# Layer-norm normalisation moved from VectorE to ScalarE, its bias made on GpSimd, under a new hand-fixed order of all engines' steps

## The reference

```python
# block 0, 16 heads of 8, EPS = 1e-5
z  = _mha(x, x, Wq1, Wk1, Wv1, mask0, causal=True)
x1 = _layernorm(x + z, ln1_g, ln1_b)
z  = _mha(x1, context, Wq2, Wk2, Wv2, mask1, causal=False)
x2 = _layernorm(x1 + z, ln2_g, ln2_b)
z  = jnp.maximum(x2 @ fc1_w.T + fc1_b, 0.0) * mask0
z  = (z @ fc2_w.T + fc2_b) * mask0
x3 = _layernorm(x2 + z, ln3_g, ln3_b)
# block 1, 16 heads of 64, eps = 1e-6; keys and values from the context
scores = qh / sqrt(dk) @ kh.T + bias + graph_attn_bias
out = softmax(scores) @ vh @ wo + bo + x3
out = (out - mu) * rsqrt(var + 1e-6) * ln_g + ln_b
```

## Time and profile before

| | |
|---|---|
| median of 3 runs | 377.48 us (376.44 to 379.8) |
| the profiled execution, its own time | 376.83 us |
| span of the profiled execution (first to last instruction) | 375.0 us |
| mean granted TensorE clock | 0.991 of full |
| busy: PE, PEld, DVE, ACT, POOL | 93%, 70%, 78%, 64%, 64% of the span |

### The profile page before, as it was taken

The page is one execution under the profiler, slowest core; times in us unless marked ns, Lnnn a source line. Parts: engine busy times, 40 slices in busy tenths (PEclk is TensorE's granted clock), DMA queues, the critical chain, the costliest instruction groups (busy, mean ns, idle before and its releaser), DMA issues.

```text
span 375.0 us, 13323 instructions
## 1 busy us (share of the span) xinstructions
PE 348.3 (93%) x5375; PEld 261.8 (70%) x5383; DVE 291.5 (78%) x836; ACT 241.2 (64%) x567; POOL 240.0 (64%) x376
## 2 busy tenths in 40 slices
PE   7588989999999999999999999999999897999998
PEld 3255547677878777777878787877688685777765
DVE  3456887898879988979889897889787966787551
ACT  1317556586767767586768776777768575577641
POOL 0243272848485859677686959596868667777763
PEclk9969999999999999999999999999999999999999
DMA  5992000020100022100102000023010010110000
GB/s 167 352 301 105 2 2 3 2 59 2 58 3 2 3 66 63 58 4 10 59 10 66 2 9 3 2 66 121 2 56 13 2 66 9 58 54 16 9 9 16
DMA packets 13181, 17.88 MB, mean 48 GB/s; under 512 B 1601, under 2 KB 10177, under 8 KB 13121
## 3 DMA queue, kind: packets, MB, share of 16 engines
q1 hardware_dynamic: 13120, 17.04, 14.7%
HBM read 15.99 MB, written 1.05 MB: 45 GB/s over the span
## 4 chain that ended last, share of the span: by engine, by line
PE 66%; DVE 9%; ACT 8%; POOL 7%; issue 5%; SPq 2%; DMA 1%; ACTq 0%; POOLq 0%; DVEq 0%
PE C_E L545 6%; PE C_E L600 6%; PE C_E L561 4%; PE C_E L590 4%; PE A_E L407 3%; PE B_E L407 3%; PE A_E L426 3%; PE C_E L577 3%; PE B_E L329 3%; PE A_E L440 2%; PE B_E L426 2%; PE C_E L502 2%; ACT qT L731 1%; PE B_J L369 1%; PE B_E L440 1%
## 5 line engine op out<-in xcount | busy, mean ns | idle before, releaser
L1039 POOL TENSOR_TENSOR Sc<-Sc,C_mx 128x512 f32<-128x512 f32 x28 | 29.1, 1043 | 33.0 <-DVE C_mx L947 33.0
L989 POOL TENSOR_TENSOR A_kblk<-A_qk,cst 128x1024 f32<-128x1024 f32 x16 | 30.3, 1896 | 17.4 <-DVE A_qk L833 17.4
L731 ACT ACTIVATE qT<-C_E,bq 128x128 f32<-128x128 f32 x112 | 31.7, 370 | 13.6 <-PE C_E L545 13.6
L999 POOL TENSOR_TENSOR L_rstd<-L_ve,cst 128x1 f32<-128x1 f32 x64 | 35.1, 549 | 5.0
L997 POOL TENSOR_TENSOR L_ve<-L_mv,cst 128x1 f32<-128x1 f32 x64 | 12.1, 189 | 39.4 <-DVE L_mv L898 38.9
L1010 POOL TENSOR_TENSOR L_xg<-L_xh,vec_sb 128x128 f32<-128x128 f32 x64 | 29.3, 458 | 11.9 <-DVE L_xh L907 11.7
L989 POOL TENSOR_TENSOR B_kblk<-B_qk,cst 128x1024 f32<-128x1024 f32 x16 | 30.3, 1897 | 2.6 <-DVE B_qk L833 2.4
L545 PE MATMUL C_E<-x3T,wq_sb 128*128 128x128 f32 x224 | 31.2, 283 | 0.0
L1048 POOL TENSOR_TENSOR Pc<-Pc,C_rd 128x512 f32<-128x512 f32 x28 | 28.9, 1042 | 2.1 <-DVE C_rd L957 1.8
L600 PE MATMUL C_E<-wo_sb,C_zT 128*128 128x128 f32 x224 | 27.9, 278 | 1.1 <-DVE Sc L937 1.1
L545 PEld LDWEIGHTS C_E<-x3T,wq_sb 128*128 128x128 f32 x224 | 27.1, 191 | 1.5 <-issue 0.6
(11 more groups left out here) (179 smaller groups left out, 1021.9 us busy)
## 6 DMA issues: line engine op xcount, KB each, us to landing
f<-in_fs SPq DMA_DIRECT2D x16, 512.0 KB, 3.7
out<-osb SPq DMA_DIRECT2D x16, 64.0 KB, 1.6
xTs<-in_xT SPq DMA_DIRECT2D x1, 768.0 KB, 9.2
xs<-in_x SPq DMA_DIRECT2D x1, 768.0 KB, 11.1
cs<-in_ctxn SPq DMA_DIRECT2D x1, 768.0 KB, 12.8
cTs<-in_ctxT SPq DMA_DIRECT2D x1, 768.0 KB, 9.3
vec_sb<-in_vecs SPq DMA_DIRECT2D x1, 640.0 KB, 6.7
wk_sb<-in_wk SPq DMA_DIRECT2D x1, 512.0 KB, 4.2
```

The source lines that it names most:

```text
L731: last = act.activation(place(n).qT[:, 4 * g + j], place(n).E[g][:, j * P:(j + 1) * P], ACT.Identity, bias=bq8[:, 4 * g + j:4 * g + j + 1] ...
L989: tt(a.kblk[:], a.qk[:, 1].unsqueeze(1).to_broadcast([P, 8, P]), at["rmask"].unsqueeze(2).to_broadcast([P, 8, P]), ALU.mult).then_inc(a.s_ ...
L999: tt(l.rstd[:], l.ve[:], at["power"], ALU.pow).then_inc(l.s_rstd, 1)
L1039: tt(v, v, place(n).mx[:, 8 * g:8 * g + 8].unsqueeze(2).to_broadcast([P, 8, S]), ALU.subtract).then_inc(C.s_sub, 1)
```

## The change

The instruction that writes `xh` goes from DVE (`tensor_scalar`, subtract and multiply) to ACT (`activation` Identity with `scale = rstd` and `bias = nb`, both one value a partition). POOL makes the bias `nb = -mean * rstd` with one more small `tensor_scalar` behind its power, so its `rstd` step has three instructions and two waits on itself. POOL's power now waits for the `xh` of the pair before (it overwrites `rstd`), and DVE's `bn_aggr` waits for `nb` of the pair before. All the numbers of `TURN`, `SHIFT` and `MOVES` are new, so the order of every engine is new. The sort that makes `PLAN` is the same.

```diff
-            l.rstd = sb(name + "_rstd", [P, 1])
+            l.rstd, l.nb = sb(name + "_rstd", [P, 1]), sb(name + "_nb", [P, 1])
...
+            def xh(l):
+                def step(n):
+                    act.wait_ge(l.s_nb, n + 1)
+                    if n:
+                        act.wait_ge(l.s_xg, n)
+                    act.activation(l.xh[:], l.y, ACT.Identity, bias=l.nb[:, 0:1], scale=l.rstd[:, 0:1]).then_inc(l.s_xh, 1)
+                return step
...
                     if n:
-                        dve.wait_ge(l.s_rstd, 2 * n)
+                        dve.wait_ge(l.s_nb, n)
                     dve.bn_aggr(l.mv[:], l.st[:]).then_inc(l.s_st, 1)
-                return step
-
-            def xh(l):
-
-                def step(n):
-                    dve.wait_ge(l.s_rstd, 2 * n + 2)
-                    if n:
-                        dve.wait_ge(l.s_xg, n)
-                    ts(l.xh[:], l.y, l.mv[:, 0:1], l.rstd[:, 0:1], ALU.subtract, ALU.mult).then_inc(l.s_xh, 1)
                 return step
...
                     pool.wait_ge(l.s_rstd, 2 * n + 1)
+                    if n:
+                        pool.wait_ge(l.s_xh, n)
                     tt(l.rstd[:], l.ve[:], at["power"], ALU.pow).then_inc(l.s_rstd, 1)
+                    pool.wait_ge(l.s_rstd, 2 * n + 2)
+                    ts(l.nb[:], l.mv[:, 0:1], l.rstd[:, 0:1], -1.0, ALU.mult, ALU.mult).then_inc(l.s_nb, 1)
                 return step
...
 TURN = """
-C.loadf=-26.883018006 C.store=-24.459548631 A.m0=-21.572682671 C.chi=-21.300857442 A.q0=-21.027749677
...
+K.warm=-66.189258692 C.whi=-59.455516873 C.wlo=-59.255277783 C.wvhi=-59.135367780 C.wvlo=-57.917225969
...
```

More of the change, by code:

```diff
@@ L179, in norm @@
             l.g, l.b, l.eps = vec[g], vec[b], eps
-            l.s_y, l.s_st, l.s_rstd, l.s_xh, l.s_xg, l.s_out = (
-                sem(name + "_" + s) for s in ("y", "st", "rstd", "xh", "xg", "out"))
+            l.s_y, l.s_st, l.s_rstd, l.s_nb, l.s_xh, l.s_xg, l.s_out = (
+                sem(name + "_" + s) for s in ("y", "st", "rstd", "nb", "xh", "xg", "out"))
             return l
@@ L755, in _ @@
                           nm + ".pts_0": pts(a, 0), nm + ".pts_1": pts(a, 1), nm + ".zts": zts(a)}
+            for k, l in (("A.", L1), ("B.", L2), ("B.3", L3), ("C.", L4)):
+                steps[k + "xh"] = xh(l)
             for g in range(2):
@@ L1072 @@
[L1072 to L1076, removed]
@@ L1087 @@
[L1087 to L1091, removed]
@@ new lines @@
+A.exp_1=-39.698980284 A.pt_0=-39.667170504 A.pt_1=-39.658426251 A.pts_0=-39.638358855 A.pts_1=-39.600689991
+A.pv_0=-39.550192019 A.pv_1=-39.505916818 A.zts=-39.479086357 C.k_0=-39.446620085 A.z=-39.420641251
+C.k_1=-39.397056866 C.ks_0=-39.386896501 C.ks_1=-39.355475904 A.y=-39.321858204 A.zn=-39.317639179
+A.st=-39.310154048 A.rstd=-39.253970807 A.xh=-39.145167601 A.gb=-38.979284281 B.cm=-38.500757520
+B.am=-38.483341845 B.tr=-38.305750131 B.xts=-38.262265725 B.qkv=-38.199907432 B.qk=-38.116663204
@@ new lines @@
+B.q0=-38.091499286 B.e0=-38.048938760 B.nz=-38.010955691 B.kblk=-37.999682825 B.cnt=-37.996832504
+B.cut=-37.958768552 B.v=-37.939922381 B.e=-37.784331587 B.max_0=-37.711340297 B.max_1=-37.697541882
+B.sub_0=-37.580379120 B.exp_0=-37.537418189 B.sub_1=-37.509380313 B.pt_0=-37.451145024 B.exp_1=-37.392169028
+B.pts_0=-37.376336410 B.pt_1=-37.330301725 B.pts_1=-37.291316697 B.pv_0=-37.226953932 B.pv_1=-37.213538689
+B.zts=-37.159859668 B.z=-37.120087902 B.zn=-37.016758988 B.y=-36.929493284 B.st=-36.876877648
@@ new lines @@
+C.fadd_0=-35.588498098 C.fadd_1=-35.565807876 C.max_0=-35.496566190 C.max_1=-35.448586860 C.sub_0=-35.444034645
+C.exp_0=-35.431102929 C.sub_1=-35.429612334 C.den_0=-35.319434976 C.nrm_0=-35.259262406 C.exp_1=-35.126969617
+C.den_1=-35.044441179 C.nrm_1=-34.941040892 C.pt_0=-34.891067718 C.pt_1=-34.891065205 C.store=-34.876879236
+C.pts_0=-34.862841496 C.pts_1=-34.793893943 C.zt=-34.771699169 C.zts_0=-34.731963894 C.zts_1=-34.690611021
+C.x3c=-34.645927740 C.o=-34.488828892 C.y=-34.385194498 C.st=-33.868785586 C.rstd=-33.751024413
@@ new lines @@
+L.warm#15=-11.098535410 A.qk#0=-23.498690921 A.qk#1=-19.802708301 A.qk#2=-19.763909938 A.qk#3=-20.224541021
+A.qk#4=-20.714710629 A.qk#5=-20.478036018 A.qk#6=-20.803214884 A.qk#7=0.230631446 A.qk#8=0.146274171
+A.qk#9=0.028211108 A.qk#10=0.130327158 A.qk#11=0.193589234 A.qk#12=0.070960346 A.qk#13=0.083425166
+A.qk#14=-0.049249739 A.qk#15=-0.046536786 C.whi#0=-0.117880345 C.whi#1=-0.224082744 C.whi#2=-0.323722276
+C.whi#3=0.100084020 C.whi#4=0.038962993 C.whi#5=0.001183341 C.whi#6=-0.009074067 C.whi#7=0.092005951
```

897 lines of the change are left out of this document (448 added, 449 removed).

## The result

The changed kernel takes 394.39 us (median of 4 runs, 392.6 to 397.53) where the kernel before takes 377.74 in the same comparison (4 runs, 376.44 to 379.8): a ratio of 1.0445 with a 95% interval of 1.0363 to 1.0526. It is 16.7 us slower. I had forecast 372.9 us, and a range up to 380.

The account below looks back on a forecast made before the run. The prediction took PE's own work to bound the middle, DVE next. Start -1.5, middle -4.0 and end +0.9 made -4.6 us: 372.2 for the profiled execution, 372.9 us for the median, range 368.5 to 380.

Parts of the forecast that it names:

- What bounds the kernel: Whole run: PE's own work bounds the middle, busy 195.8 of 200 us, with DVE next.
- The relief of DVE: DVE: 64 xh instructions taken away, 25 us of its 291.5 us busy time.
- Added on ACT and POOL: ACT: 64 ACTIVATEs of 0.47 us, 30 us at most; POOL: 64 nb of 0.19 us, 17 us with gaps.
- The latency of a norm: Each norm, variance to xh: 0.34 us longer, plus what stands before it in ACT's queue.
- the two waits that look back one pair: Power for the last xh, aggregate for the last nb: costed at nothing, in the middle and near the last pairs.
- Rival (b): ACT's and POOL's queues take over, PE waits 16 x 0.34 = 5.4 us for chain B's xh: 382.3 us; chance 0.15.
- The start, -1.5: Start, to 84.85 us: some six places gain 0.1 to 0.5 us each, 1.5 us taken; bounds 0 and 2.8.
- The middle, -4.0: Middle, 11 periods: relieved DVE and periodic order remove the irregular part, a gain of 4.0 us; bounds 0 and 5.3.
- the likeliest case: Whole run: the forecast's own case, gain of 7.6 to 2.5 us, 369.9 to 375.0 us; chance 0.48.
- rival (d): Order worse by 0.2 us a period, DVE's relief pays: 376.9 us; chance 0.27, shared with the rival of a hidden gain.
- The end, +0.9: End, from 308.23 us: three longer norms +1.0, more idle products +0.4, B.nz earlier -0.5: 0.9 us longer.
- rival (c): Start, 19 to 25 us: the drop to half clock goes too, giving 370.5 us; chance 0.10.

Follow-up runs that it names:

- dve_xh_late: Kernel before with 55 of the 64 xh one place later in VectorE's own queue, nothing else changed: 390.36 us, ratio 1.0328.
- edit_alone: The edit (xh on ScalarE, nb on GpSimd) under the order of the kernel before, only xh given places in ScalarE's queue: 394.21 us, ratio 1.0418.
- order_alone: New order on every engine with the code of the kernel before, xh on VectorE at places chosen by the author: 391.75 us, ratio 1.0328.
- act_no_nb: Kernel before's order, xh moved to ScalarE, no nb (constant bias, mean not subtracted): 390.0 us, ratio 1.0313.
- dve_after_nb: As pool_nb, but VectorE's xh waits for nb and uses it: 388.59 us, ratio 1.0269.
- pool_nb: Kernel before's code and order, GpSimd also makes the 64 nb, awaited only by the same norm's next aggregate: 382.08 us, ratio 1.0112.
- act_l2: Kernel before's order; only norm L2 (after attention B) has xh on ScalarE and nb on GpSimd: 383.94 us, ratio 1.0197.
- new_start: Kernel before's code, steps grouped in the new order's three pieces, only the first in the new order inside: 385.59 us, ratio 1.0206.
- act_l4: Kernel before's order; only the fourth norm (before the output) has xh on ScalarE and nb on GpSimd: 378.69 us, ratio 1.003.
- new_end: Kernel before's code, steps grouped in the new order's three pieces, only the last in the new order inside: 381.6 us, ratio 1.0111.

## Why the prediction was wrong, step by step

**What bounds the kernel.** "The middle of the run is bound by PE's own work", with DVE next, was read from shares. PE's share was right and the conclusion from it wasn't. dve_xh_late adds no work to any engine and is 12.7 us longer; so PE's 98% is the outcome of an order and no cushion in which a norm's delay is lost. "PE itself waited for xh hardly at all there: 0.2 us" is the same error. I read a wait of nothing as slack. It only says that PE wasn't made to wait, with that order, by that `xh`; it gives no figure for how much later `xh` may come, and none for the steps that stand behind it in its engine's queue.

**The relief of DVE.** I had 25 us off and 266 us left; it is 274.8, so 16.7 off. The 64 durations do add up to 25. But instructions of one engine overlap in the trace: the `xh` at 52.34 lasts to 52.75 and `A_mx` behind it began at 52.67, so what an `xh` takes up is less than its duration. With the order held fixed it is 0.29 to 0.30 us: DVE has 272.8 us in edit_alone for 291.5 before, and 274.8 after for 294.2 in order_alone. The other 2.7 us of the difference to before are the new order's. The term that follows from it was wrong in kind, not only in size: "what can be won in the middle is what a late DVE costs". act_no_nb has all of the relief (272.6 us) and none of the `nb`, and it loses 12.2 us.

**Added on ACT and POOL.** The ACTIVATE (0.47 for 0.46 to 0.50) was right; `nb` was set too low (0.19 for 0.264), and the busy sums were near: ACT 264.5 for 268, POOL 256.3 for 252. The rule of the Trainium skill, page "ScalarE: Activation LUTs", section "Rules for kernel authors", that an add or multiply belongs on VectorE, I weighed and set aside by the occupancies. The measured result is on the side of the Trainium skill: the move alone costs 3.1%. The price of the instruction, for which I had cited it, doesn't explain that much, though: 48 x 0.06 + 16 x 0.15 = 5.3 us, if all of it fell on the chain, for 12.2 measured.

**The latency of a norm.** Computed as 0.34 us; with the measured pieces it is 0.264 + 0.08 + 0.06 = 0.40. The sum of the forecast has this term at the end (3 x 0.34) and nowhere else. In the middle it stands at nothing, and no reason is given for that: this is the step that failed most plainly. dve_after_nb against pool_nb gives 6.5 us for it, with `xh` still on DVE. The queue of ACT is named in the same paragraph ("for which PE waits") and gets no term either; act_no_nb gives 12.2 us for the move. What I did cost at nothing in words, the two waits that look back one pair, was right: neither shows up as a wait in the trace after.

Rival (b) came nearest, with a chance of 0.15. Its sign, waits of PE or ACT behind `xh` of more than 3 us in sum, was there: 5.4 us at PE's energy product of chain B alone. Its size was luck where it fits. It took 16 x 0.34 = 5.4 us for one norm, L2, in every pair; the 6.5 us of dve_after_nb are those of all four norms, and PE waited at that product in 7 pairs, not 16. Its 382.3 us were short of 394.4, since it had nothing for POOL's time (4.3 us), nothing for ACT's stops and nothing for the order; and my range ended at 380, below its own number. L2 is indeed the dearest norm (act_l2, 7.5 us), but L1 and L3 cost 4.4 and 4.8, so it isn't one norm's matter.

**The start, -1.5.** Measured +3.75. "Such a place gives 0.1 to 0.5 us" counted the places where an `xh` leaves DVE and none where one arrives on ACT. new_start shows 5.3 us lost by the order of this piece alone.

**The middle, -4.0 (bounds 0 and 5.3).** Measured +11.1: this is most of the miss. The bounds themselves failed, for I let the middle only stay or gain (and the range of the likeliest case used 3.4 as the least gain, where the section had 0). "A relieved DVE and a periodic order take away the irregular part" has two halves, and both failed. The relief didn't pay: act_no_nb has it and is slower, and act_l4, whose norm no engine waits for but the store, takes 4.4 us off DVE (287.1 for 291.5) and is no faster (1.003). The new order of the middle costs 8.1 us with before's code, 20.9 us a period for 20.3; it is only a little more periodic than before's, and I hadn't counted that. Nor was "PE's order is nearly the same in both" true: it was read off one period, and 337 of PE's 577 steps have another place. My rival (d) had the order's price with 0.2 us a period and DVE's relief paying for it; it was 0.6, and nothing paid. What in the new order costs the time stays open.

**The end, +0.9.** Measured +2.6; new_end puts the part of the order at some 1.3, within its interval. The 27 trailing products are there: the last piece of the chain after is

```profile
386.35 5.83 PE B_E L329 x27
```

5.83 us for my 5.8. The sign was right and so were these 5.8; the size was short by 1.7. Behind the end of the last `C.o` the time grew by 0.9 us (6.05 for 5.11), and in front of it by 1.6, where I had +1.0 for three norms and -0.5 for DVE's place; no run tells these two apart, and none took the six added products away.

**The clock, rival (c).** The half speed from 19 to 25 us is gone, at 1.00 in all of these slices; and another came, after the hole of PE at 52 to 54 us. Three stretches of 1 us after (PEclk third from the end):

```profile
24.00:25.00 1.00, 0.16 (x4) 0.19 (x8) 0.00 (x0) 0.46 (x1) 0.36 (x2) 1.00 1.19 276
...
53.00:54.00 1.00, 0.00 (x0) 0.00 (x0) 1.00 (x4) 0.52 (x2) 0.75 (x2) 1.00 0.03 8
...
57.00:58.00 1.00, 1.00 (x5) 0.89 (x4) 1.00 (x4) 0.96 (x2) 0.00 (x0) 0.50 0.00 0
```

PE had 0.21 us of work between 52 and 54, and stood at 1.2 GHz (0.50) from about 56 to 60. So (c) came true as written and brought nothing: a low clock at one place was exchanged for one at another, and the mean granted clock is 0.991 in both profiles. Its price can be read from the other executions of the kernel before in these comparisons. Twelve of them had a mean granted clock of 1.000, with a median of 376.2 us, and 28 had 0.991, with 377.6: 1.4 us between them, for the 2.4 that I had worked out.

**The order and the edit together.** Under before's order the edit costs 16.6 us. Under the new one it costs 2.6 by the medians (394.39 for 391.75), but the intervals of the two ratios overlap (1.0363 to 1.0526 and 1.0254 to 1.0401), and order_alone's places of `xh` were mine. What can be said is that the costs don't add up, and that the new order with the edit is no better than before's with it (394.2). Whether the new order is a good one for the edit, beside other orders for it, stays open.

## What to carry to other kernels

In a kernel whose order is written out and worked off in order by every engine, a wait of nothing in the profile isn't slack: 0.2 us were shown for `xh` here, and one place later in its queue cost 12.7. Move the step one place later in a run, and see how far that moves it in time, before anything is costed at nothing. Moving work to an emptier engine is to be priced by the latency that it adds to its chain and by its place in the new queue (too early stops the queue, too late stops the reader), and only then by the share of busy time that it frees. A new order is an edit of its own and wants a measurement of its own, and a word for it ("periodic", "nearly the same") is to be counted on the lists before anything is built on it.

## What was not expected of the hardware

POOL's 128x1 multiply with two scalars (`nb`, one of them a column of 128x1) takes 0.264 us where its 128x1 add of two columns takes 0.190 in the same trace: small instructions of the same tile aren't alike there. ACT's ACTIVATE with two such columns takes 0.496 us from SBUF and 0.458 to 0.465 from PSUM; on DVE the same normalisation was faster from SBUF (0.350 for 0.404). And busy time isn't the sum of durations. Under before's order, 64 instructions with 25 us in sum took 18.7 us off DVE's busy time, and the 64 on ACT, 30 us in sum, added 23.3 to ACT's (241.2 to 264.5, in edit_alone). That is 0.10 us less than its duration for each ACTIVATE (0.13 under the new order, 243.0 to 264.5). The Trainium skill, page "ScalarE: Activation LUTs", section "What ACT_TABLE_LOAD costs", has successive ACTIVATEs overlap by some 93 ns; these sums, over ACTIVATEs of which some stood behind idle time, agree with that in size.
